# Decoder layer on one core: row maxima and context rows turned by 32x32 block transposes and small transfers in place of matrix products, with the steps in another order

## The reference, cut to what matters

```python
x = x + local_attn(layernorm(x))       # 16 heads of 16, window of 7 tokens
x = x + cross_attn(layernorm(x), ctx)  # 16 heads, keys and values from the 120 context rows
h = layernorm(x)
y = h + causal_attn(rmsnorm(h, n1))    # 16 heads, 256 x 256, causal
y = y + moe(rmsnorm(y, n2))            # 256 -> 1024 (silu) -> 256, times a gate factor
out = x + y
```

## Time and profile before

| what | value |
| --- | --- |
| median of three runs | 3522.82 us (3520.79 to 3526.21) |
| the profiled execution, its own time | 3523.18 us |
| its span, first to last instruction | 3521.5 us |
| PE busy | 3464.6 us, 98% |
| DVE busy | 2674.4 us, 76% |
| POOL busy | 2498.7 us, 71% |
| ACT busy | 1828.8 us, 52% |
| granted TensorE clock, mean | 0.999 |

### The profile page before, as it was taken

The page is one execution under the profiler, slowest core; times in us unless marked ns, Lnnn a source line. Parts: engine busy times, 40 slices in busy tenths (PEclk is TensorE's granted clock), DMA queues, the critical chain, the costliest instruction groups (busy, mean ns, idle before and its releaser), DMA issues.

```text
span 3521.5 us, 92506 instructions
## 1 busy us (share of the span) xinstructions
PE 3464.6 (98%) x36557; PEld 2788.9 (79%) x36557; DVE 2674.4 (76%) x5867; ACT 1828.8 (52%) x4241; POOL 2498.7 (71%) x3160
## 2 busy tenths in 40 slices
PE   8899999999999999999999999999999999999998
PEld 5577888888888888888888888888888888888876
DVE  5677787787787787787787787787787787787763
ACT  3344555555555555555545545545545545545542
POOL 5767777777777777777777777777777777777731
PEclk9999999999999999999999999999999999999999
DMA  5111221121121121221121221221221121121200
GB/s 182 50 51 50 70 73 51 68 74 51 68 74 52 67 74 50 69 74 50 66 77 47 69 77 46 69 77 47 69 77 47 69 77 47 69 77 47 69 8 10
DMA packets 90151, 223.35 MB, mean 63 GB/s; under 512 B 9286, under 2 KB 56706, under 8 KB 73346
## 3 DMA queue, kind: packets, MB, share of 16 engines
q1 hardware_dynamic: 89730, 217.44, 18.1%
HBM read 164.92 MB, written 50.39 MB: 61 GB/s over the span
## 4 chain that ended last, share of the span: by engine, by line
PE 94%; POOL 2%; ACT 2%; DVE 2%; issue 1%; SPq 0%; DMA 0%; DVEq 0%; POOLq 0%; ACTq 0%
PE ps L970 13%; PE ps L961 13%; PE ps L832 11%; PE ps L810 10%; PE ps L888 9%; PE ps L939 9%; PE ps L866 9%; PE ps L911 8%; PE ps L838 5%; PE ps L790 3%; PE ps L860 1%; PE ps L877 1%; ACT prob L1075 1%; PE ps L925 1%; POOL chunks L635 1%; DVE nmax L1407 1%
## 5 line engine op out<-in xcount | busy, mean ns | idle before, releaser
L635 POOL TENSOR_TENSOR chunks<-v_windows,xT 128x560 f32<-128x560 f32 (+1 forms) x384 | 879.6, 2301 | 92.2 <-DVE xT L1382 89.2
L1407 DVE TENSOR_REDUCE nmax<-ps 128x4 f32<-128x480 f32 (+2 forms) x1280 | 776.9, 671 | 182.8 <-PE ps L866 182.6
L1075 ACT ACTIVATE prob<-ps 128x256 f32<-128x256 f32 (+2 forms) x1536 | 670.7, 556 | 457.7 <-PE ps L888 457.5
L630 POOL TENSOR_TENSOR chunks<-rest,k_windows 128x512 f32<-128x512 f32 (+1 forms) x384 | 552.2, 1455 | 373.9 <-DMA k_windows<-passed_on 301.1
L1361 DVE TENSOR_REDUCE held<-chunks 128x80 f32<-128x560 f32 (+1 forms) x384 | 294.6, 768 | 321.2 <-POOL chunks L635 319.8
L961 PE MATMUL ps<-xT,w_up 128*128 128x256 f32 x2048 | 480.3, 383 | 1.4 <-ACT xT L1028 1.3
L970 PE MATMUL ps<-w_down,held 128*128 128x256 f32 x2048 | 459.1, 382 | 1.1 <-DVE held L1460 1.0
L970 PEld LDWEIGHTS ps<-w_down,held 128*128 128x128 f32 x2048 | 383.8, 190 | 60.1 <-DVE held L1460 2.8
L961 PEld LDWEIGHTS ps<-xT,w_up 128*128 128x128 f32 x2048 | 372.4, 190 | 69.4 <-issue 20.6
L1232 POOL TENSOR_SCALAR_AFFINE_SELECT prob<-prob 128x512 f32<-128x512 f32 x512 | 311.3, 642 | 50.6 <-ACT prob L1075 50.6
L1028 ACT COPY xT<-ps 128x512 f32<-128x512 f32 x256 | 152.9, 597 | 361.6 <-PE ps L790 361.6
(11 more groups left out here) (152 smaller groups left out, 6783.8 us busy)
## 6 DMA issues: line engine op xcount, KB each, us to landing
k_windows<-passed_on SPq DMA_DIRECT2D x64, 1024.0 KB, 5.0
v_windows<-passed_on SPq DMA_DIRECT2D x64, 1024.0 KB, 5.0
x<-in_x SPq DMA_DIRECT2D x64, 256.0 KB, 2.9
passed_on<-rest SPq DMA_DIRECT2D x64, 256.0 KB, 2.3
passed_on<-held SPq DMA_DIRECT2D x64, 256.0 KB, 3.7
out<-x SPq DMA_DIRECT2D x64, 256.0 KB, 2.2
y<-in_ctx SPq DMA_DIRECT2D x64, 120.0 KB, 2.9
held<-nmaxT SPq DMA_DIRECT2D x256, 8.0 KB
```

What stands on the lines that cost most here:

```text
L630: return engine.tensor_tensor(chunk_of(c).rearrange("p (j d) -> p j d", d=D), token_rows["q"][s][:, b, :].unsqueeze(1).to_broadcast([P, n, ...
L635: return engine.tensor_tensor(chunk_of(c).rearrange("p (h i j) -> p h i j", i=HD, j=WINDOW), window("v", b * D + first * HD, (HD, n), (1, ...
L1075: last = nc.scalar.activation(prob_pair(seq, L, m)[0:keys, :, r, col:col + qs], of_pair, ACT.Exp, scale=SCALE)
L1407: nc.vector.tensor_reduce(of_heads[:, ms[0]:ms[-1] + 1, :, r], src, AX_X, ALU.max, negate=True).then_inc(emptied[b], 1)
```

## The change

Three things are changed. The step `shift` leaves TensorE: DVE writes the maxima into a padded tile `max_blocks` (per partition 2 x 2 blocks of 32 columns, 8 of them used) and turns that tile by 32x32 blocks; `place` then takes the rows out of the blocks with eight DMAs of 4 rows instead of two of 8. The step `turn_ctx` leaves TensorE and ACT: DVE turns the context rows in place by 32x32 blocks (`flip`), four DMAs (`spread`) write the blocks into a DRAM tensor so that they come to stand turned (runs of 32 numbers, 128 bytes), and one DMA (`gather`) reads it back. The tables that set the order are new, and with them the order on every engine. Some paths that were switched off (`EARLY = 0`) are taken out. At the start DVE clears 32 rows of the context tile of each lane before it gives the signal for which SP's first DMA waits.

```diff
+BY_DMA = ("ctx",)
+FLIP, SPREAD_KB = 0.56, 1000
...
-POSITION = {("turn", (0,)): -0.0773, ("turn_ctx", ()): -0.0394, ("project_rows", ("k",)): -0.0389, ("project_rows",
...
+POSITION = {("turn", (0,)): 0.5152, ("project_rows", ("k",)): 0.6146, ("project_rows", ("v",)): 0.8394,
...
+    def by_dma(what, after, flip, hops, spread_kb, kb):
+        a = part("flip", (what,), "DVE", flip, after)
+        a = part("spread", (what,), "SP", hops * DMA_ISSUE, [a, of_ctx] if what == LOCAL and of_ctx else [a],
+                 lag=LANDING, kb=spread_kb)
+        return part("gather", (what,), "SP", DMA_ISSUE, [a], lag=LANDING, kb=kb)
...
-                source = through("turn_ctx", (), 0.22, "ACT", 0.27, [loaded])
+                source = of_ctx or through("turn_ctx", (), 0.22, "ACT", 0.27, [loaded])
...
-            a = through("shift", (layer,), 0.2, "DVE", 0.4, last)
-            shifted = part("place", (layer,), "SP", 2 * DMA_ISSUE, [a], lag=2.0)
+            a = part("shift", (layer,), "DVE", 0.2, last)
+            shifted = part("place", (layer,), "SP", 8 * DMA_ISSUE, [a], lag=1.6)
...
-        nmaxT = per_lane("nmaxT", [H, T])
+        nmaxT = per_lane("nmaxT", [P, 4 * SLOT])
+        max_blocks = per_lane("max_blocks", [P, 2, 2, SLOT])
...
+        features = nc.dram_tensor("features", (LANES, D, T), F32).ap()
+        ctx_features = nc.dram_tensor("ctx_features", (LANES, D, P), F32).ap()
...
-                        wait_taken(sp, "shift", seq, L)
+                        sp.wait_ge(flipped[s], reached["flipped", "shift", seq, (L,)])
                         for e in range(2):
-                            to = qT[s][e][16 * (1 - e):P:32]
-                            sp.dma_start(to, nmaxT[s][8 * e:8 * e + 8, :]).then_inc(placed[s], 16)
+                            to = qT[s][e][16 * (1 - e):P:32].rearrange("r m (b i q) -> r m b i q", b=2, q=SLOT)
+                            for i in range(4):
+                                first = SLOT * i + 4 * e
+                                sp.dma_start(to[:, :, :, i, :], nmaxT[s][first:first + 4, :]).then_inc(placed[s], 16)
+                    elif name == "spread":
+                        what, = args
+
+                        sp.wait_ge(flipped[s], reached["flipped", "flip", seq, args])
+                        if what == "ctx":
+                            to = ctx_features[s].rearrange("(x f) t -> f x t", f=SLOT)
+                            for first in range(0, C, SLOT):
+                                last = min(first + SLOT, C)
+                                sp.dma_start(to[:, :, first:last], ctx_blocks[s][first:first + SLOT, :, 0:last - first]
+                                             ).then_inc(spread[s], 16)
...
+                    elif name == "gather":
+                        what, = args
+
+                        sp.wait_ge(spread[s], reached["spread", "spread", seq, args])
+                        if what == "ctx":
+                            sp.dma_start(cT[s], ctx_features[s].rearrange("(k p) t -> p k t", p=P)[:, :, 0:C]
+                                         ).then_inc(gathered[s], 16)
...
-                    elif name == "shift":
-                        L, = args
-                        wait_taken(pe, "max", seq, L, len(max_fills(L, T, C)) - 1)
-                        b = bank(name, seq, args)
-                        for tb in range(2):
-                            last = nc.tensor.transpose(ps[0:H, b, tb * P:(tb + 1) * P], nmax[s][:, tb, :], ident[:])
-                        last.then_inc(filled[b], 1)
...
+                for s in range(LANES):
+                    nc.vector.memset(cx[s][3 * SLOT:P, :], 0.0)
                 nc.vector.memset(zero_rows, 0.0).then_inc(filled_ones, 1)
...
+                    elif name == "flip":
+                        what, = args
+                        if what == "ctx":
+                            dve.wait_ge(ctx_loaded[s], reached["ctx_loaded", "load", seq, ()])
+                            rows = cx[s]
...
+                        nc.vector.transpose(rows, rows).then_inc(flipped[s], 1)
...
                     elif name == "shift":
-                        b = bank(name, seq, args)
-                        nc.vector.tensor_copy(nmaxT[s][:], ps[0:H, b, 0:T]).then_inc(emptied[b], 1)
+                        L, = args
+                        for f in range(len(max_fills(L, T, C))):
+                            wait_taken(dve, "max", seq, L, f)
+                        nc.vector.transpose(nmaxT[s][:], max_blocks[s][:].rearrange("p m b h -> p (m b h)")).then_inc(
+                            flipped[s], 1)
```

202 lines of the change are left out of this document (111 added, 91 removed).

## The result

The changed kernel takes 3476.4 us in the median of four runs (3475.73 to 3479.07); the kernel before, run beside it, 3524.1. The medians are 47.7 us apart; the ratio is 0.9868, with a 95% interval of 0.9856 to 0.9879: 1.3% faster. Forecast were 3510 us, with a range from 3488 to 3548.

A forecast was written before the change was run, and what follows sets the result against it. The prediction took TensorE to bound the kernel: 3523.2 us, -21.6 for TensorE's own work, -4.3 at start and end, +12 for the new wait, gave 3509, stated as 3510 us. The range was 3488 to 3548.

The forecast's parts named there:

- TensorE is the bound, and 41.0 us leave it: TensorE, busy 599.22 of 600 us: two `shift` and one `turn_ctx` fewer in each of 64 sequences, 41.0 us less.
- What the order puts back: TensorE's new step order: 12.1 us for more excursions and 7.3 us for returns, leaving -21.6 us net.
- excursion: TensorE going from whole-array steps into divided steps and back: 0.22 us each, 55 more of them, 12.1 us.
- the return: First whole-array step behind divided ones on TensorE, where `shift` stood before: 0.11 us more in 66 places, 7.3 us.
- The new wait, +12: TensorE's cross `scores` 1 waiting for the longer `place`: 0.2 us per cycle over 60 cycles, +12 us.
- `scores` at +9.8 and `place` at +9.95: Layout in us from the end of cross `max` 1: cross `scores` 1 comes at +9.8, `place` has landed at +9.95.
- Start and end, -4.3: Outside the regular cycles: -8.7 for fewer passing products, +1.4 for DVE's clearings, +3 for the longer `place`.
- fewer passing products: Products with which TensorE fills waits at start and end: 36 fewer at 0.241 us, -8.7 us.
- Small pieces in DRAM: Rival: 1024 pieces of 128 bytes or less per sequence from `spread` delay window fetches and `place`; 3560 us, chance 5%.
- A fixed part of a DMA: `place` on SP: the skill's 2.0 us would add 9 us to the sum; the row's at most 1.8 was used.
- its lowest case: No new wait on TensorE and the full gain at the start: 3494 us, below 3498, chance 14%.

The follow-up runs named there:

- the second table change: Kernel before with one table number changed, `up` moved between `gate` and causal `scores`, one more excursion into divided steps: 3568.0 us.
- old means in the new order: Kernel before, both turns still on TensorE, with the changed kernel's order tables: 3515.3 us.
- the run with half of `place`: Changed kernel with four of the eight transfers of `place` left out: 3469.6 us.
- The two spare ones above: Changed kernel with two more four-row transfers to DRAM, read by nobody, in SP's queue ahead of the eight of `place`: 3546.3 us.

## Why the prediction was right and wrong

- **TensorE is the bound, and 41.0 us leave it: right.** In the new order the means are worth 38.9 us, 0.64 in the shortest distance.
- **"What the order puts back", 12.1 + 7.3 us: one half of the account is missing.** One more excursion costs 0.09 in the shortest distance, or 0.15 in the second table change, and not 0.22 and the return besides. On whole-array steps the price is there: added up from start to start over cycles of the shortest distance, they take 36.78 us before and 37.03 with the old means in the new order, 0.25 more. The return shows too: four `up` take 3.55 us behind `shift` and 3.65 in the changed kernel. But the steps divided by rows fell, from 11.13 to 10.98, and to 10.82 in the changed kernel, and the sum had put them at nothing. Over 64 cycles 0.09 is 6 us where 19 were put: 13 of the error. What shortens the divided steps wasn't settled. It is not a dearer change from columns to rows in the old cycle, which the expectations name. Causal `max` 0 does take 1.28 us before (1238.18 to 1239.46 in the earlier trace rows, behind `values`) and 1.17 after (1223.00 to 1224.17, behind a whole-array step), but the 0.11 lies at its end: its last eight products take 0.32 where whole-array `shift` follows and 0.23 where `scores` follows (1223.94 to 1224.17). The row of before:

```profile
1239.14 0.39 PE L866 MATMUL ps<-rest,held 32*128 32x128 f32 x8
```

- **The new wait, +12: in size wrong, in place right.** In the regular cycle there is none. By the run with half of `place` it costs 7 us over the whole program, as irregular waits. The layout was close: `scores` at +9.8 and `place` at +9.95 were forecast, and counted from 1214.21, where cross `max` 1 ends, they came at +9.96 and +9.87. TensorE came later because local k took 2.04 us where 1.84 was laid out. That `place` costs the regular cycle nothing is so by a tenth of a microsecond, and partly luck. Here some 5 of the error.
- **Waits that the old order had: missed.** I took the cycle of before as if it had none but its steps. Its mean stood 0.18 above its shortest distance, and the new order took 0.15 of it away (52.83 to 52.86 with the old means). 64 times 0.15 is some 10 us that the prediction had no term for. They were in sight: the distances of the `down` rows in the same view as the earlier trace rows.
- **Start and end, -4.3: too small.** 13.7 us were gained at the start, 1.9 lost at the end. The reason given, fewer passing products, isn't borne out (48 and 71 fewer saved nothing); the order alone gives 9.6 at the start (375.35 to 365.71). What in it does so wasn't settled.
- **Small pieces in DRAM: right to be held unlikely.** 104,448 packets more raised the share of the earlier trace rows from 18.1 to 20.8%: 0.208 x 16 x 3475.1 - 0.181 x 16 x 3521.5 = 1367 us over 16 engines, 0.013 us a packet, where 0.114 had been taken as the mean. With the context on TensorE the queue has 107,138 packets at 18.1%, so the added time is that of the context's way. The Trainium skill (DMA: Bandwidth & Descriptors, Specifications) says that transfers below 512 bytes are read, modified and written; if these were, it cost nothing that the page of the profile shows. Each of the four transfers of `spread` landed in a median of 1.6 to 1.7 us.
- **A fixed part of a DMA.** In the chains the last transfer of `place` lands 1.6 us after its issue starts (1.66 above) and 1.1 after it ends, by the rows not the 2.0 us that the Trainium skill (DMA: Bandwidth & Descriptors, Anatomy of one DMA) gives for one from GpSimd; to go by the row was right.

Together 13 + 5 + 10, and 7.5 us at start and end, are 35.5 us; the forecast missed by 33.6. The sum is not exact: the first three are reckoned over 64 cycles, start and end over what lies outside 56, so eight cycles count twice. The range failed on the low side since its lowest case still had the full price of the excursions and no gain from waits.

## What to carry to other kernels

Before a cycle is priced step by step, compare its shortest with its mean distance: what lies between are waits, and a new order can take them away or bring them; here they were 10 of the 34 us that the forecast missed. When the price of a boundary between two kinds of steps is read from rows, both sides belong to it. A change of means and a change of order are one change when a step's transfers get longer: tried apart, one of them lost 76 us and the other gained 9. A step that leaves an engine also gives back the buffer that it filled, and that was worth more than a third of what the context's turn cost in the cycle. And where a queue works in order, look at what stands ahead of the waiting transfers: a 0.4 us instruction on an engine with idle time, moved behind another, cost 63 us, because four transfers of somebody else's waited for it in the same queue.

## What the runs showed of the hardware

- The eight transfers of 4 rows by 512 bytes take 4.64 us of SP's time, 0.58 each, the two of before, of 8 KB, 0.55: the issue doesn't get cheaper with a quarter of the bytes. The two spare ones above, also 4 rows of 512 bytes but to DRAM and row by row, took 0.26 and 0.30 us where `place` cuts its rows into pieces of 128 bytes in SBUF: the shape or the place of the destination sets the length, which of the two wasn't tried.
- A block transpose by DVE took 0.30 us for 128 x 128 and 0.41 to 0.43 for 128 x 256.
- The transfer of the local keys to DRAM, issued 0.80 us behind `gather` (1223.85 after 1223.05), has a median landing of 3.7 us in the changed kernel and 2.3 in the kernel before, 2.0 where the context stays on TensorE. That the two close together in one queue delay each other is my reading of these rows; no run tried it alone. First the changed kernel's page, then that of the one with the context on TensorE (KB, median us to landing):

```profile
passed_on<-rest SPq DMA_DIRECT2D x64, 256.0 KB, 3.7
```

```profile
passed_on<-rest SPq DMA_DIRECT2D x64, 256.0 KB, 2.0
```
